# A six-stage decoder kernel: finer blank fills, full 32-column value strips, blocks without a GpSimd drain, and a causal stage whose maxima are subtracted on GpSimd

## The reference

```
x = layernorm(x + taylor_attention(x))              # linear attention, 8 heads of 16
x = layernorm(x + cross_attention(layernorm(x), ctx))   # 16 heads of 64, 77 keys, gated ("wide")
x = layernorm(x + gelu_experts(x))                  # 8 experts, top 2
x = layernorm(x + causal_attention(x))              # 16 heads of 8, 128 keys, slopes and causal mask
x = layernorm(x + cross_attention_with_rotation(x, ctx))  # 16 heads of 8, 77 keys ("rotary")
x = layernorm(x + swiglu_experts(x))                # 8 experts, top 2, and a shared one
```

## Time and profile before

| | us |
|---|---|
| median of 3 runs | 2891.46 (2889.1 to 2892.21) |
| profiled execution: its own time | 2890.11 |
| profiled execution: span of its profile | 2888.3 |
| taylor stage | 0 to 226.5 of the span |
| wide stage | 226.5 to 1044.6 |
| gelu experts | to 1375 |
| causal stage | to 1927 |
| rotary stage | to 2534.3 |
| swiglu experts | from 2543.7 to the end |

### The profile page before, as it was taken

One profiled execution on the slowest core, in us unless ns is written; L12 is line 12 of the kernel. 1 busy time (PEld: TensorE's weight loads), 2 busy tenths in 40 slices (PEclk: granted clock), 3 DMA queues, 4 the chain that ended last, 5 costly groups with the idle time before them and its releaser, 6 DMA issues. The chain is left out here.

```text
span 2888.3 us, 63045 instructions
## 1 busy us (share of the span) xinstructions
PE 2554.6 (88%) x19424; PEld 1891.0 (65%) x19424; DVE 1952.0 (68%) x5426; ACT 1830.7 (63%) x5343; POOL 1441.1 (50%) x1852
## 2 busy tenths in 40 slices
PE   8998979799798639997899999968999999779996
PEld 6666757578576539995455555546766666547994
DVE  6884757677577635556688888876677777434655
ACT  6773646566465324444799999957888888622334
POOL 4442324445455445554333333326678888723775
PEclk9998989999899869999899999989999999889998
DMA  9923464745747222224010000000000000011336
GB/s 264 338 75 97 153 204 153 245 144 155 241 138 231 86 66 72 71 69 132 12 58 9 11 9 11 9 25 7 17 26 28 29 28 21 26 33 42 92 93 190
DMA packets 274488, 267.96 MB, mean 93 GB/s; under 512 B 29740, under 2 KB 253241, under 8 KB 273776
## 3 DMA queue, kind: packets, MB, share of 16 engines
q1 hardware_dynamic: 256592, 228.42, 26.1%
q0 software_dynamic: 17280, 34.13, 3.5%
q10 hardware_dynamic: 288, 1.38, 0.1%
HBM read 101.24 MB, written 151.85 MB: 88 GB/s over the span
## 5 line engine op out<-in xcount | busy, mean ns | idle before, releaser
L758 POOL TENSOR_TENSOR wide_probs<-wide_exps,wide_inv_sum 128x616 f32<-128x616 f32 x128 | 168.3, 1315 | 385.8 <-DVE wide_inv_sum L1538 299.9
L1248 ACT ACTIVATE causal_exps<-causal_biased,causal_neg_max 128x128 f32<-128x128 f32 x1024 | 325.8, 391 | 31.1 <-DVE causal_neg_max L1552 29.6
L739 POOL DMA_INDIRECT sorted_x<-send,place_i x240 | 244.8, 1020 | 91.7 <-issue 34.9
L1248 ACT ACTIVATE rotary_exps<-banks,rotary_neg_max 128x77 f32<-128x77 f32 x1024 | 251.9, 351 | 15.1 <-DVE rotary_neg_max L1552 14.7
L1050 PE MATMUL banks<-wide_folded,wide_probsT 128*128 128x128 f32 x1280 | 191.1, 281 | 78.1 <-issue 71.7
L1050 PEld LDWEIGHTS banks<-wide_folded,wide_probsT 128*128 128x128 f32 x1280 | 172.0, 197 | 80.4 <-issue 77.6
L1799 ACT ACTIVATE gelu_hidden<-banks,gelu_slot 128x256 f32<-128x256 f32 x284 | 116.7, 471 | 157.1 <-PE banks L1976 157.1
L1499 DVE TENSOR_TENSOR causal_biased<-banks,regions 128x512 f32<-128x512 f32 x256 | 164.6, 685 | 72.2 <-PE banks L1074 69.8
L1730 POOL DMA_INDIRECT results<-gelu_tile_out,gelu_dest_i x142 | 140.2, 987 | 142.4 <-DVE gelu_tile_out L1886 120.1
L1552 DVE TENSOR_REDUCE rotary_neg_max<-banks 128x4 f32<-128x308 f32 x256 | 121.6, 475 | 119.4 <-PE banks L1088 114.6
L1730 POOL DMA_INDIRECT results<-swiglu_tile_out,swiglu_dest_i x142 | 144.2, 1015 | 115.8 <-DVE swiglu_tile_out L1881 60.6
(11 more groups left out here) (384 smaller groups left out, 7214.5 us busy)
## 6 DMA issues: line engine op xcount, KB each, us to landing
v_dram<-wide_staged SPq DMA_DIRECT2D x38, 1024.0 KB, 4.9
sorted_x<-blank SPq DMA_DIRECT2D x1, 34848.0 KB, 116.8
sorted_x<-blank SPq DMA_DIRECT2D x4, 8712.0 KB, 30.6
wide_folded<-v_dram SPq DMA_DIRECT2D x128, 256.0 KB
gelu_tile_in<-sorted_x SPq DMA_DIRECT2D x71, 132.0 KB, 2.1
swiglu_tile_in<-sorted_x SPq DMA_DIRECT2D x71, 132.0 KB, 2.1
gelu_back<-results SPq DMA_DIRECT2D x16, 512.0 KB, 8.0
swiglu_back<-results SPq DMA_DIRECT2D x16, 512.0 KB, 6.0
```

Source lines behind the costliest of these rows:

```text
L739: pool.indirect_dma_start(route["sorted_x"], bass.IndirectOffsetOnAxis(ap=r_place_i[:, b % 2, which, n // 2:n // 2 + 1], axis=0), send[:, ...
L758: pool.tensor_tensor(probs[:, half % SLOTS, 0:HH * NK].rearrange("p (k h) -> p h k", h=HH), exps[:, half % EB], inv_sum[:, half % SLOTS].u ...
L1248: last = act.activation(exps[:, (NU * c.c + k) % ES, h], scores[:, h * NK:(h + 1) * NK], ACT.Exp, bias=neg_max[:, k % SLOTS, h:h + 1])
```

## The change

Six edits, made together.

1. **Finer fill.** `FILLS` goes from 4 to 24. The DMAs leave `load` and are issued one for each pair, for pairs 4 to 27 of the wide stage, after that pair's `store_chunk` and `load_folded`.
2. **Strips.** The two late stages add two heads into one strip of 32 rows: the values of odd heads lie 16 columns further right, and PE accumulates an even and an odd head in PSUM. A sequence then fills 256 columns of one bank. It is copied to `sums` once instead of twice, on ACT in both stages, and `turn_back` has two transposes instead of four. The rotary stage takes the heads in the order that the causal one has.
3. **No drain.** All blocks are opened with `no_gpsimd_drain=True`. The barrier stays.
4. **Causal: joint output transposes.** Both sequences of a pair are transposed in one go at slot 7 (`turn_outputs`), and copied by one ACT instruction (`keep_outputs`) instead of two. The projection, the residual addition and what follows move one slot later (`OT_LAG` = 1).
5. **Causal: maxima on GpSimd.** A new POOL instruction for each slot, `take_max`, adds `neg_max` to `biased` and writes `exps`, one slot after the maximum. ACT makes one exponential of the whole slot in place, two slots after the scores. DVE's rings `biased` and `neg_max` are released by `take_max` (semaphore `lessened`) and no longer by the exponential.
6. **Causal: later transposes.** `TLAG`, `PLAG`, `OLAG` go from 2, 3, 4 to 3, 4, 5 in the causal stage; the value projection of the front moves behind the weighted sum in its slot.

```diff
-FILLS = 4
+FILLS = 24
-        block = ctx.enter_context(nc.Block())
+        block = ctx.enter_context(nc.Block(no_gpsimd_drain=True))
+            def blank_part(n):
+                rows, cleared, blank = fill
+                size = SORTED_ROWS // P // 2 // FILLS
+                sp.dma_start(rows.rearrange("(p j k) d -> p j (k d)", p=P, k=2)[:, size * n:size * (n + 1)],
+                             blank.unsqueeze(1).to_broadcast([P, size, 2 * ROW])).then_inc(cleared, 16)
+
             def step(f, ahead=None, pair=None):
                 if f is not None:
                     load(f)
                 if kind == "wide" and pair is not None:
                     values_step(pair.c)
+                    if 4 <= pair.c < 4 + FILLS:
+                        blank_part(pair.c - 4)
...
+            def take_max(pair, m):
+                pool.wait_ge(max_done, pair.count(NU, m + 1))
+                if before(pair, m, ES) is not None:
+                    bc, bk = before(pair, m, ES)
+                    pool.wait_ge(probsT_ps, bc.count(NU, bk + 1))
+                pool.tensor_tensor(exps[:, (NU * pair.c + m) % ES], biased[:, m % BS].rearrange("p (h n) -> p h n", h=HU),
+                                   neg_max[:, m % SLOTS].unsqueeze(2).to_broadcast([P, HU, NK]), ALU.add).then_inc(lessened, 1)
...
+                    if kind == "causal" and lagged(c, u, k, 1) is not None:
+                        take_max(*lagged(c, u, k, 1))
                     if kind != "wide":
                         keys_ahead(pool, f, c, k, POOL_KEYS)
...
-        TLAG, PLAG, OLAG = (2, 3, 4) if late else (4, 5, 6)
+        TLAG, PLAG, OLAG = {"wide": (4, 5, 6), "causal": (3, 4, 5), "rotary": (2, 3, 4)}[kind]
...
-                for n in range(NC):
-                    at = first_head(n) * STRIP
-                    last = pe.transpose(f_bank[:, at:at + P], sums[:, b, n * P:(n + 1) * P], ident)
+                for n in range(2):
+                    last = pe.transpose(f_bank[:, n * P:(n + 1) * P], sums[:, b, n * P:(n + 1) * P], ident)
                 last.then_inc(back_ps, 1)
+
+            def late_sum(pair, n):
+                b, j = divmod(n, UB)
+                g, odd = divmod(j, 2)
+                pe.wait_ge(probsT_done, pair.count(NU, n + 1))
...
+                for h in range(HU):
+                    strip = 272 * 2 * b + 256 * odd + 32 * (4 * g + h)
+                    last = pe.matmul(o_bank[b][32 * h:32 * h + 32, g * P:(g + 1) * P], values[0:NK, pair.c % 2, strip:strip + 32],
+                                     probsT[0:NK, n % 2, h * P:(h + 1) * P], start=odd == 0, stop=odd == 1)
+                last.then_inc(pv_done, 1)
...
+            def turn_outputs(u):
+                pe.wait_ge(norm_done, u.count(2, 2))
+                if u.c >= 1:
+                    pe.wait_ge(z_done, u.c)
+                for b in range(2):
+                    last = pe.transpose(y_bank[:, b * P:(b + 1) * P], o[:, b].rearrange("p h d -> p (h d)"), ident)
+                last.then_inc(oT_ps, 1)
...
+                    if kind == "causal" and lagged(c, u, k, 2) is not None:
+                        pair, m = lagged(c, u, k, 2)
+                        act.wait_ge(lessened, pair.count(NU, m + 1))
+                        e_slot = exps[:, (NU * pair.c + m) % ES]
+                        act.activation(e_slot, e_slot, ACT.Exp).then_inc(exps_done, 1)
...
+                    if late and at is not None and at[1] % UB == UB - 1:
+                        pair, b = at[0], at[1] // UB
+                        act.wait_ge(pv_done, pair.count(NU, at[1] + 1))
                         if pair.back(1).real:
                             act.wait_ge(back_ps, pair.back(1).count(2, b + 1))
-                        act.activation(sums[:, b, j * P:(j + 2) * P], o_bank[(m // 2) % 2][:, 0:2 * P], ACT.Copy).then_inc(o_done, 1)
+                        act.activation(sums[:, b], o_bank[b][:, 0:2 * P], ACT.Copy).then_inc(o_done, 1)
...
-                    dve.wait_ge(exps_done, bc.count(NU, bk + 1))
+                    dve.wait_ge(lessened, bc.count(NU, bk + 1))
...
-                            dve.wait_ge(exps_done if late else shifted_done, bc.count(NU, bk + 1))
+                            dve.wait_ge(shifted_done if kind == "wide" else lessened if kind == "causal" else exps_done, bc.count(NU, bk + 1))
...
-                    if kind == "causal" and at is not None and at[1] % 2 == 1:
...
-                        dve.tensor_copy(sums[:, b, j * P:(j + 2) * P], o_bank[(m // 2) % 2][:, 0:2 * P]).then_inc(o_done, 1)
```

More of the change, by code:

```diff
@@ L436, in softmax_attention @@
         xT = sb("xT", [P, 2, 2, P])
-        if kind != "wide":
-            values = sb("values", [P, 2, 2, H, STRIP])
+        if late:
+            values = sb("values", [P, 2, STRIPS])
         keys = sb("keys", [P, 2, H, 2, NK] if kind == "wide" else [P, 2, KH, NK])
@@ L659, in load @@
                         sp.dma_start(into, source).then_inc(landed, 16)
-                if fill is not None and f.c % (n_pairs // FILLS) == n_pairs // FILLS - 1:
-                    rows, cleared, blank = fill
-                    n = SORTED_ROWS // P // 2 // FILLS
-                    part = slice(n * (f.c // (n_pairs // FILLS)), n * (f.c // (n_pairs // FILLS) + 1))
-                    sp.dma_start(rows.rearrange("(p j k) d -> p j (k d)", p=P, k=2)[:, part],
-                                 blank.unsqueeze(1).to_broadcast([P, n, 2 * ROW])).then_inc(cleared, 16)
             run_steps(sp, step, n_pairs, 3 if kind == "wide" else 1, 4)
@@ L721, in _ @@
                 pool.wait_ge(ready, 4)
-                pool.memset(values[:, :, :, :, D:D + 1], 1.0).then_inc(ready, 1)
+                for s in range(2):
+                    last = pool.memset(value_heads(s)[:, :, :, D:D + 1], 1.0)
+                last.then_inc(ready, 1)
             chip.clear_old(pool)
@@ L1110, in step @@
                     if at is not None and late:
-                        pair, n = at
-                        b, j = divmod(n, UB)
-                        g = n // 2
-                        pe.wait_ge(probsT_done, pair.count(NU, n + 1))
-                        if n == 0:
-                            pe.wait_ge(front_done, pair.count(FU, FU))
-                        if n % 2 == 0 and before(pair, n, 4) is not None:
-                            bc, bk = before(pair, n, 4)
-                            pe.wait_ge(o_done, bc.count(OG, bk // 2 + 1))
-                        for h in range(HU):
-                            chunk, row = divmod(STRIP * h, P)
-                            col = ((n % 2) * CU + chunk) * P
-                            last = pe.matmul(o_bank[g % 2][row:row + STRIP, col:col + P], values[0:NK, pair.c % 2, b, first_head(j) + h],
-                                             probsT[0:NK, n % 2, h * P:(h + 1) * P], start=True, stop=True)
-                        last.then_inc(pv_done, 1)
+                        late_sum(*at)
                     if f is not None:
@@ L1129, in step @@
                         unit(units_at(f, c, k))
-                    if late:
-                        if u is not None and k in (6, 7):
-                            turn_output(u, k - 6, ranked)
-                        if mine is not None and k == 0:
-                            project_late(mine)
+                    if kind == "causal" and u is not None and k == 7:
+                        turn_outputs(u)
+                    if kind == "rotary" and u is not None and k in (6, 7):
+                        turn_output(u, k - 6, ranked)
+                    if late and mine is not None and k == OT_LAG:
+                        project_late(mine)
             if route is not None:
@@ L1205, in step @@
                 for k in range(NU):
-                    if late and mine is not None and k == 0:
+                    if kind == "causal" and mine is not None and k == 0:
+                        keep_outputs(mine)
+                    if kind == "rotary" and mine is not None and k == 0:
                         keep_output(mine, 1)
@@ L1240, in step @@
                         act.activation(exps[:, half % EB], exps[:, half % EB], ACT.Exp).then_inc(exps_done, 1)
-                    if c is not None and late:
+                    if kind == "causal" and lagged(c, u, k, 2) is not None:
[3 more added lines that the diff above has]
+                        act.activation(e_slot, e_slot, ACT.Exp).then_inc(exps_done, 1)
+                    if c is not None and kind == "rotary":
                         act.wait_ge(max_done, c.count(NU, k + 1))
-                        scores = biased[:, k % BS] if kind == "causal" else s_bank[k % 2]
+                        scores = s_bank[k % 2]
                         if before(c, k, ES) is not None:
@@ L1512, in step @@
                 for k in range(NU):
-                    if late and n is not None and k == 1:
+                    if late and n is not None and k == 1 + OT_LAG:
```

(4 more changed lines are left out.)

63 lines of the change are left out of this document (34 added, 29 removed).

## The result

The changed kernel takes 2842.56 us (median of 4 runs, 2841.36 to 2844.71) where the kernel before took 2891.84 (median of 4 runs, 2889.1 to 2892.94): a ratio of 0.9832, with a 95% interval of 0.9815 to 0.9849. That is 49 us faster, not the 127 forecast, and 28 us above the upper end of the range. Its profiled span is 2840.1 us, that of the kernel before 2888.3.

The account below looks back on a forecast made before the run. PE was taken to bound the wide stage outside four fills and the rotary stage, ACT and PE the causal one. 75 + 10 + 13 + 29 = 127 off 2890.1 gave 2763, median 2764 us; range 2725 to 2815.

Parts of the forecast that it names:

- The step that failed: Causal stage: ACT falls from 15.29 to 10.8 us and bounds no more; DVE's and POOL's lists give about 15.1 a pair.
- the term of 29 us: Causal stage: pair from 16.60 to 15.6 us, 32 us won less 3 for a deeper pipeline at its ends.
- Rival A: Causal stage gains nothing, as DVE-POOL hand-offs with two buffers idle POOL 0.3 us each; 2793 to 2806 us; chance 0.2.
- its bound of 17.0: Causal stage: slow bound of the pair's period, 17.0 us, with 13 us lost.
- The 13 us lost at 17.0: Causal stage: loss given for the slow bound, a pair of 17.0 us.
- Rivals B: Wide stage: pieces of fill still delay the reload by 1.5 us on each of 24 steps; 2797 us; chance 0.1.
- D: Wide stage: every reload and store waits for a whole piece, PE restarts slowly; 7.3 us a step, 2936 us; chance 0.03.
- a term of 13: Rotary stage, strips: pair from 16.13 to about 15.7 us, 0.4 x 32 = 13 us won; bounds 0 and 27.
- The bound of 15.0: Causal stage: fast bound of the pair's period, 15.0 us, with 48 us won.
- The 15.04: Causal stage: PE's forecast busy time a pair in us, after saving 0.44 from 15.48.

Follow-up runs that it names:

- the ring of four: Changed kernel with four tiles of maxima in the causal stage where there were two: 2840.89 us, ratio 0.9818.
- the trail of two: Changed kernel with causal transposes, sums and what follows, and fronts, one slot later, and five exponential buffers: 2730.94 us, ratio 0.9443.
- the exponential first: Changed kernel with the causal exponential moved ahead of the copy of the transposed weights in ACT's list: 2770.56 us, ratio 0.9576.
- the trail of one in the kernel before: Kernel before with causal transposes, weighted sums and kept sums at one, two and three slots instead of two, three and four: 3119.08 us.
- the exponential first and the ring of four: Changed kernel with the causal exponential ahead of the copy and four tiles of negated maxima: 2765.93 us, ratio 0.9571.
- all three edits: Changed kernel with causal transposes trailing the exponential by two slots, the exponential ahead of the copy, and four tiles of maxima: 2734.72 us, ratio 0.9447.

## Why the prediction was wrong

- **The step that failed** is in the causal part: ScalarE "goes to ... 10.8 and is no bound any more", and then "Following both lists through eight slots gives about 15.1 us a pair". The lists followed were VectorE's and GpSimd's. ScalarE was left out because its busy time was low, and TensorE's list was not followed either. ScalarE's busy time was forecast well (11.03), but not its place in a chain. The diff showed all of it: lags from 2 to 3, the exponential from slot 0 to 2, so the trail from two slots to one. The prediction counts the pipeline as two slots deeper at its ends, but nowhere holds the lag of the transposes against the exponential's own move. Followed through ScalarE's and TensorE's lists, a turn of 0.62 + 0.66 + 0.60 us with nothing of its own beside it comes to 1.9, eight of them to 15.0, and each to more wherever scores or fronts stand in it; measured, they come to 18.18, and the term of 29 us won became 55 lost.
- **Rival A** gave "causal gains nothing" by hand-offs between VectorE and GpSimd, at most 17.0. Both the mechanism and the size were wrong: the ring of four moved nothing, and the period was 18.18. Hence the range missed too: its bound of 17.0 came from the same two engines. (The 13 us lost at 17.0 also leave out the 3 for the deeper pipeline, which the other bound has.)
- **The sizes of the pieces held.** `take_max` took 1.04 (1.09 forecast), the exponential 0.62 (0.61), GpSimd was busy 13.69 (14.4), VectorE 12.88 (13.5). VectorE's two writes of `X` took 0.62 each on average where I gave each 1.13; these 1.0 us are more than the 0.6 by which VectorE fell short.
- **The rule of the Trainium skill** ("SBUF — State Buffer", section "SBUF: two separate sides"), by which such a write, met by a GpSimd instruction under way, is blocked until that one ends, would give up to 0.34 + 1.04 a write, an estimate with the durations of this case. The two writes of the pair shown in the changed kernel took 0.80 and 0.48, the 64 on average 0.62. The trace agrees that the writes take longer beside GpSimd than the 0.34 alone; a wait for a whole `take_max` at each of them it does not show. Nor does GpSimd's busy share tell the price: with the trail of two GpSimd is busy for 13.67 of 14.78, and the writes took 0.36 on average. The causal period did not hang on it.
- **Joint output transposes** were costed at nothing. That is right where ScalarE was the busiest engine (period 16.59 without the moved maxima). In the changed kernel it was the second thing missed: with edit 4 VectorE's residual addition waits for the projection at the head of its list, and moving the projection one slot later took 0.65 us off the pair. The wait that the prediction did look at, TensorE's for both divisions, is 11.1 us in 350 with the exponential first, 0.5 a pair, as forecast.
- **Finer fill** was right in mechanism and nearly in size: 81 alone (75 to 85), where 75 was taken and 78 was the bound. The pieces cost nothing that shows, so the charge for them was not needed (24 x 0.1 is 2.4, where 3 was taken); the four long intervals were worth 78.6, not the 80.5 of waits and restarts. Rivals B and D are out.
- **No drain** was right: 10.7 measured, 10 taken, and the run with this edit alone shows the drain as the cause, which the trace of before could not.
- **Strips in the rotary stage** were right: the run without drain alone has 606.5 us there, the changed kernel 592.1, so 14.4 for a term of 13; the early pair takes 15.70, as forecast. Of the other runs with strips some are up to 8 us longer there (last section).
- **The bound of 15.0** was too high as a floor. With a full trail the causal pair takes 14.78. The 15.04 was taken off a busy time that has waits in it (last section).

## What to carry to other kernels

A lag must be counted from the instruction that makes the operand, not from the head of the pipeline: when a producer moves two slots later, its consumers move two slots later as well, or the slack between them is gone. Busy time tells about how short a period can't be; it does not tell that an engine with little of it is no bound. The Trainium skill ("Perfetto Trace Analysis", section "Identifying the Most-Contended Engine") calls the engine with the highest occupancy the most contended one, to be optimized first, and judges TensorE's headroom by other measures than its busy time. In the changed kernel GpSimd leads the other engines with 13.69 of 18.18, and TensorE's modelled 15.23 is above it; the work of neither bound the pair, so here occupancy did not find the bound. Before an edit to a software pipeline is priced, follow the lists of every engine in the loop, and look above all for an instruction that waits for another engine's answer to the instruction just ahead of it in its own list. Here the order of two instructions was worth 72 us, the missing slot with the shifts around it 112, and the change that looked like a loss of 55 us in its stage was a gain of 59 (551.7 to 493.0) once its lags and the slots around them were right.

## What the runs showed of the hardware

- The busy time of TensorE depends on its waits: the same 134 recorded matmuls of a causal pair count 15.23 us in the changed kernel (18.18 a pair), 15.21 with the exponential first (16.06) and 14.69 with the trail of two (14.78). Of the eight groups of four transposes in a pair, none counts under 0.65 in the changed kernel, and three count 0.60 with the trail of two. So TensorE's busy time of a stretch with waits is no floor for its period. The Trainium skill ("Perfetto Trace Analysis", section "Tensor Engine Instruction (MATMUL, LD_WEIGHTS)") says that the ends of TensorE's instructions are estimated and not observed. The traces fit that; they can't show an end.
- In the records a `Copy` on ScalarE lets the next instruction of its list begin before it ends: 0.60 long, followed by the exponential 0.49 later (1579.84 and 1580.33). A chain worked out from durations laid end to end is too long by some 0.1 us at such a link.
- The end of a block after scatters cost 10.7 us in two places together: without GpSimd's drain GpSimd's list shows no wait there, and VectorE starts the next block 2.5 us before GpSimd's last scatter of the block before is through.
- The granted clock can fall where TensorE waits: with the trail of one in the kernel before, a pair in which TensorE is busy for 15.89 of 22.53 us keeps 1.00, but twelve of 29 pairs come out at 0.93 or 0.87 and take 24.0 to 25.6. In the changed kernel, with 15.23 of 18.18, it is 1.00 throughout the steady part of the stage (1350 to 1880).
- The rotary stage, whose code is the same in all versions with strips, took from 592.0 to 599.8 us (the first with the exponential first and the ring of four, the last with all three edits). These 8 us lie in four pairs of the second: 20.14 and 18.63 us where the first has 18.27 and 17.20, and 18.50 and 21.10 where it has 16.94 and 16.96. The granted clock is 0.98, 0.93, 0.91 and 0.76 in these four and 1.00 in the first run's; in the pair of 20.14 TensorE also waits 1.9 us for ScalarE's `rotary_oT`, against 0.2. Why this happens in some runs is not shown.
